# Self-attention's output projection as three float32r products, with in-place cosine products

## The reference

```python
q = (xn @ Wq).reshape(b, n, h, dh).transpose(0, 2, 1, 3)
k, v = split(xn @ Wkv)
q = q * cos + _rotate_half(q) * sin
k = k * cos + _rotate_half(k) * sin
attn = softmax(where(causal, neg, einsum('bhid,bjd->bhij', q * scale, k)))
out = einsum('bhij,bjd->bhid', attn, v).transpose(0, 2, 1, 3).reshape(b, n, h * dh)
x = x + out @ Wo                       # 2048 x 256: the output projection
x = x + cross_attention(layernorm(x), ctx)
x = x + ffn(layernorm(x))
```

## Time and profile before

| | |
|---|---|
| median of 3 runs | 1405.72 us (1403.78 to 1406.74) |
| the profiled execution | 1405.16 us, of which its span 1403.3 us |
| busy over the span | PE 1383.5 us (99%), PEld 1169.1, DVE 975.1 (69%), ACT 716.2 (51%), POOL 437.1 (31%) |
| block A | from 0 to about 362 us |
| block B | from 362.2 us to the end |
| output projection (L710) | 512 instructions, 32 for each of 16 pairs |

### The profile page before, as it was taken

How to read it: one execution, slowest core, us unless ns; L and a number is a source line. 1 busy time by engine, 2 the same in 40 slices (tenths; PEclk the granted TensorE clock), 3 DMA queues, 4 the chain that set the end, 5 groups by cost and what they waited for, 6 DMA issues and landing times.

```text
span 1403.3 us, 55347 instructions
## 1 busy us (share of the span) xinstructions
PE 1383.5 (99%) x25185; PEld 1169.1 (83%) x25185; DVE 975.1 (69%) x1824; ACT 716.2 (51%) x940; POOL 437.1 (31%) x433
## 2 busy tenths in 40 slices
PE   8999999999999999999999999999999999999997
PEld 6788888876788888888888888888888888888884
DVE  5776677666246768677777768677777767676766
ACT  3545445443455555555465555555465555555450
POOL 4333233222223233323333233323323233324310
PEclk9999999999999999999999999999999999999999
DMA  9100000000211121211212121211212121211100
GB/s 255 37 1 32 1 31 1 31 1 2 68 53 49 33 76 51 60 50 47 65 32 66 33 78 50 61 50 47 65 32 65 32 79 50 61 50 47 50 4 8
DMA packets 38923, 66.78 MB, mean 48 GB/s; under 512 B 3717, under 2 KB 36930, under 8 KB 38690
## 3 DMA queue, kind: packets, MB, share of 16 engines
q1 hardware_dynamic: 38690, 63.24, 15.7%
HBM read 61.40 MB, written 1.84 MB: 45 GB/s over the span
## 4 chain that ended last, share of the span: by engine, by line
PE 72%; DVE 2%; issue 0%; POOL 0%; DVEq 0%
PE proj_ps L1366 20%; PE proj_ps L1357 20%; PE score_ps L1384 14%; PE sum_ps L1409 13%; PE side_ps L1444 2%; PE side_ps L1458 1%; PE side_ps L1426 1%; PE side_ps L1451 1%; DVE amax L1245 0%; DVE hidden L1267 0%; DVE sig L1277 0%; DVE hidden L1278 0%; PE side_ps L1433 0%; DVE exps L1167 0%; DVE totals L1189 0%
## 5 line engine op out<-in xcount | busy, mean ns | idle before, releaser
L1119 ACT ACTIVATE exps<-score_ps 125x1792 f32<-125x1792 f32 x192 | 320.4, 1669 | 431.1 <-PE score_ps L1384 431.1
L1167 DVE TENSOR_SCALAR exps<-exps,top 125x896 f32<-125x896 f32 x384 | 288.1, 792 | 22.1 <-ACT exps L1119 17.5
L1384 PE MATMUL score_ps<-spread,keys 32*125 32x112 f32 x6144 | 219.0, 279 | 0.0
L1158 DVE COPY vals<-proj_ps 125x512 f32<-125x512 f32 x192 | 129.5, 688 | 116.6 <-PE proj_ps L1366 114.3
L1409 PEld LDWEIGHTS sum_ps<-exps,vals 125*32 125x32 f32 x12288 | 162.4, 110 | 46.9 <-issue 34.0
L1384 PEld LDWEIGHTS score_ps<-spread,keys 32*125 32x125 f32 x6144 | 184.8, 183 | 15.4 <-issue 0.3
L1409 PE MATMUL sum_ps<-exps,vals 125*32 125x56 f32 x12288 | 190.9, 214 | 0.0
L1049 POOL TENSOR_TENSOR low<-raw_early,high 128x500 fp32r<-128x500 f32 x64 | 84.5, 1322 | 216.8 <-PE proj_ps L1357 215.9
L1111 ACT ACTIVATE keys<-proj_ps,b_k 128x500 f32<-128x500 f32 x192 | 129.9, 677 | 23.7 <-PE proj_ps L1357 20.3
L1049 POOL TENSOR_TENSOR low_early<-raw_early,high_early 128x500 fp32r<-128x500 f32 x62 | 89.4, 1459 | 168.8 <-PE proj_ps L1357 168.8
L293 POOL TENSOR_TENSOR swapped<-swapped,sin 128x448 f32<-128x448 f32 (+1 forms) x72 | 86.0, 1198 | 126.5 <-ACT swapped L530 125.5
(11 more groups left out here) (169 smaller groups left out, 2415.2 us busy)
## 6 DMA issues: line engine op xcount, KB each, us to landing
raw_early<-in_ctxT SPq DMA_DIRECT2D x64, 500.0 KB, 4.1
raw<-in_ctxT SPq DMA_DIRECT2D x32, 500.0 KB, 3.6
w_q<-in_attn_Wq SPq DMA_DIRECT2D x4, 512.0 KB, 8.6
w_o<-in_attn_Wo SPq DMA_DIRECT2D x1, 2048.0 KB, 21.7
out<-y_out SPq DMA_DIRECT2D x16, 112.0 KB, 2.7
rows<-in_x SPq DMA_DIRECT2D x1, 1344.0 KB, 17.4
raw_early<-in_ffn_gate_wT SPq DMA_DIRECT2D x1, 1024.0 KB, 9.4
raw_early<-in_ffn_val_wT SPq DMA_DIRECT2D x1, 1024.0 KB, 5.1
```

What stands on the lines that cost most here:

```text
L1119: nc.scalar.activation(exps[t % 2][:, :, :, :].rearrange("p h r n -> p r h n"), score_ps[0:TILE, :, 0:2 * QW].rearrange("p r (h n) -> p r ...
L1158: nc.vector.tensor_copy(vals[r][:, 2 * q:2 * q + 2, :, 0:HD], proj_ps[q][0:TILE, :].rearrange("p (k h d) -> p k h d", k=2, d=HD))\
L1167: nc.vector.tensor_scalar(tile, tile, LIMIT_LO, top[:, n, at:at + 1], ALU.max, ALU.min)\
L1384: ins = nc.tensor.matmul(score_ps[0:TILE, r, to:to + HE * S], keys[c % 2][32 * r:32 * r + 32, k, (at + half) * TILE:(at + half + 1) * TILE ...
```

## The change

`outT` and `w_o` are each kept as two float32r tensors, a rounded half (`outT_h`, `w_oh`) and the rest (`outT_l`, `w_ol`), and the projection sums three products of them. ScalarE's `out_half` writes the rounded half, both batch rows of a half k one behind the other; a new step of VectorE, `out_low`, subtracts it from the bank, and that step now increases `outT_ready`. `attn_Wo` is loaded in three pieces into room that is unused until pair 2 (`queries`, `gate_q`), and in pair 0 ScalarE rounds it and VectorE takes the rest (`out_weights` on each). `cosines` writes its product straight into `qT` or `keyT`, and `rotated` adds in place; `by_cos` goes. To make room, the float32 cross-attention weights and the mask share the room of `w_q`, loaded after its last use; six parameters of block B are loaded at its start.

```diff
-        w_o = sb("w_o", [P, AH, D])
+        w_oh = sb("w_oh", [P, AH, D], F32R)
+        w_ol = sb("w_ol", [P, AH, D], F32R)
-        outT = sb("outT", [P, AH, ROWS])
+        outT_h = sb("outT_h", [P, AH, ROWS], F32R)
+        outT_l = sb("outT_l", [P, AH, ROWS], F32R)
...
             sp.wait_ge(raw_used, 3)
-            for c in range(2):
-                sp.dma_start(early.ring(c), context_chunk(dram, c)).then_inc(early_ctx_in[c], 16)
+            sp.dma_start(early.ring(0), context_chunk(dram, 0)).then_inc(early_ctx_in[0], 16)
+            sp.wait_ge(unit_filled, UNIT[("q", GROUPS - 1, AU - 1)] + 1)
+            for k, name in enumerate(("xattn_WkT", "xattn_WvT")):
+                sp.dma_start(early.w_f[:, k, :, :], dram[name].rearrange("(c p) n -> p c n", p=P)).then_inc(early_w_in, 16)
+            sp.dma_start(early.mask_i, dram["mask"]).then_inc(early_in, 16)
+            sp.dma_start(early.ring(1), context_chunk(dram, 1)).then_inc(early_ctx_in[1], 16)
...
                 else:
                     dve.wait_ge(swap_ready, r + 1)
-                if r >= 2:
-                    dve.wait_ge(rot_ready, r - 1)
-                chain.inc(nc.vector.tensor_tensor(by_row(by_cos[r % 2][:, 0:w]), by_row(bank(name)[:, 0:w]),
-                                                  cos[:, :].unsqueeze(1).to_broadcast([P, n, S]), ALU.mult))
-                chain.wait()
+                    nc.vector.tensor_tensor(qT[g % 2][:, name[2], :, :, 0:S].rearrange("p b h s -> p h b s"),
+                                            bank(name)[:, 0:2 * GR].rearrange("p (h b s) -> p h b s", h=2, s=S),
+                                            cos[:, :].unsqueeze(1).unsqueeze(1).to_broadcast([P, 2, GROUP, S]),
+                                            ALU.mult).then_inc(cos_ready, 1)
+                dve.wait_ge(cos_ready, r + 1)
                 nc.vector.sem_inc(free(name), 1)
...
+            def out_low(p, k, b):
+
+                dve.wait_ge(outT_high, 2 * (2 * p + k) + b + 1)
+                nc.vector.tensor_tensor(outT_l[:, AU * k:AU * (k + 1), b * S:(b + 1) * S],
+                                        out_ps[:, b, 0:AU * S].rearrange("p (h s) -> p h s", s=S),
+                                        outT_h[:, AU * k:AU * (k + 1), b * S:(b + 1) * S].bitcast(F32),
+                                        ALU.subtract).then_inc(outT_ready, 1)
+
+            def out_weights(n):
+
+                dve.wait_ge(wo_high, n + 1)
+                nc.vector.tensor_tensor(out_part(w_ol, n), out_raw(n), out_part(w_oh, n).bitcast(F32), ALU.subtract)\
+                  .then_inc(wo_low, 1)
...
                 if p:
                     norm2_rows(p - 1)
+                out_low(p, 0, 0)
+                out_low(p, 0, 1)
                 for name in more[3:4]:
                     rotary(name)
+                out_low(p, 1, 0)
+                out_low(p, 1, 1)
+                if p == 0:
+                    for n in range(len(O_PARTS)):
+                        out_weights(n)
...
+                if p == 0:
+                    for n in range(len(O_PARTS)):
+                        out_weights(n)
                 probs_out(p, 0)
                 for name in more[2:3]:
                     swap(name)
                 out_half(p, 0, 0)
+                out_half(p, 0, 1)
                 probs_out(p, 1)
-                out_half(p, 0, 1)
...
                 to = begin(("y", p))
-                pe.wait_ge(wo_in, 16)
+                pe.wait_ge(wo_low, len(O_PARTS))
                 pe.wait_ge(outT_ready, 4 * (p + 1))
                 for h in range(AH):
-                    ins = nc.tensor.matmul(to[0:ROWS, 0:D], outT[:, h, :], w_o[:, h, :], start=(h == 0),
-                                           stop=(h == AH - 1))
+                    for n, (x, w) in enumerate(((outT_h, w_oh), (outT_h, w_ol), (outT_l, w_oh))):
+                        ins = nc.tensor.matmul(to[0:ROWS, 0:D], x[:, h, :], w[:, h, :], start=(h == 0 and n == 0),
+                                               stop=(h == AH - 1 and n == 2))
```

More of the change, by code:

```diff
@@ L230, in block_a, with out_part, out_raw, wait_rotated @@
         ROT = {name: n for n, name in enumerate([name for name in units if name[0] in ("kv", "q")])}
+        O_PARTS = ((0, 8), (8, 14), (14, 16))
+        def out_part(w, n):
+            return w[:, O_PARTS[n][0]:O_PARTS[n][1], :].rearrange("p h n -> p (h n)")
+        def out_raw(n):
+            if n == 2:
+                return gate_q[:, 0, :].bitcast(F32)
+            return queries[:, :, :].rearrange("p c n -> p (c n)")[:, D * O_PARTS[n][0]:D * O_PARTS[n][1]]
+        def wait_rotated(eng, r):
+            eng.wait_ge(rot_ready, r + 1)
         def bank(name):
@@ L252, in _ @@
             sp.dma_start(rows[:, 2 * GP:PAIRS, :], x[:, 2 * GP:PAIRS, :]).then_inc(x_in[1], 16)
-            sp.dma_start(w_o[:, :, :], dram["attn_Wo"].rearrange("(h p) n -> p h n", p=P)).then_inc(wo_in, 16)
+            for n, (first, last) in enumerate(O_PARTS):
+                sp.dma_start(out_raw(n).rearrange("p (h n) -> p h n", n=D),
+                             dram["attn_Wo"].rearrange("(h p) n -> p h n", p=P)[:, first:last, :]).then_inc(wo_in, 16)
             sp.dma_start(w_xq[:, :, :], dram["xattn_WqT"].rearrange("(c p) n -> p c n", p=P)).then_inc(small2_in, 16)
@@ L262, in _ @@
                 if n == 0:
[L263 to L266, removed]
+                    sp.wait_ge(early_zero, 1)
                     for to, of in early.loads(dram):
@@ L550, in out_half, with out_weights @@
                 act.wait_ge(pv_done, 2 * p + k + 1)
-                ins = nc.scalar.copy(outT[:, AU * k:AU * (k + 1), b * S:(b + 1) * S],
-                                     out_ps[:, b, 0:AU * S].rearrange("p (h s) -> p h s", s=S))
-                ins.then_inc(outT_ready, 1)
+                nc.scalar.copy(outT_h[:, AU * k:AU * (k + 1), b * S:(b + 1) * S],
+                               out_ps[:, b, 0:AU * S].rearrange("p (h s) -> p h s", s=S)).then_inc(outT_high, 1)
+            def out_weights(n):
+                act.wait_ge(wo_in, 16 * len(O_PARTS))
+                nc.scalar.copy(out_part(w_oh, n), out_raw(n)).then_inc(wo_high, 1)
             def normed2_out(p):
@@ L667, in scores @@
                 g, j = divmod(p, GP)
-                pe.wait_ge(rot_ready, ROT[("kv", g)] + 1)
+                wait_rotated(pe, ROT[("kv", g)])
                 if p:
@@ L845, in __init__, with share @@
         self.res = sb("res", [ROWS, 1])
[L846 to L850, removed]
+    def share(self, room):
+        n = 2 * DC * D
+        self.w_f = room[:, 0:n].rearrange("p (k c n) -> p k c n", k=2, c=DC)
+        self.mask_i = room[0:TILE, n:n + BATCH * BT].bitcast(I32).rearrange("p (b t) -> p b t", b=BATCH)
     def ring(self, n):
@@ L855, in loads @@
     def loads(self, dram):
-        pairs = [(self.mask_i[:, :, :], dram["mask"]),
-                 (self.b_k[:, :], dram["xattn_bk"]),
+        pairs = [(self.b_k[:, :], dram["xattn_bk"]),
                  (self.head_of[:, :], dram["c_head_of"]),
@@ L1014, in _ @@
             load(2, 0, 2)
+            late = ((w_xo[:, :, :], dram["xattn_WoT"].rearrange("(a p) n -> p a n", p=P)),
+                    (ln_gamma[:, :], dram["xattn_gamma"].partition_broadcast(ROWS)),
+                    (ln_beta[:, :], dram["xattn_beta"].partition_broadcast(ROWS)),
+                    (gate_b[:, :], dram["ffn_gate_b"].partition_broadcast(ROWS)),
+                    (val_b[:, :], dram["ffn_val_b"].partition_broadcast(ROWS)),
+                    (out_b[:, :], dram["ffn_out_b"].partition_broadcast(ROWS)))
+            assert len(late) == N_LATE
+            for to, of in late:
+                sp.dma_start(to, of).then_inc(late_in, 16)
             def store(p):
```

56 lines of the change are left out of this document (28 added, 28 removed).

## The result

The changed kernel takes 1428.18 us (median of 4 runs, 1426.83 to 1428.37) against 1406.23 before: the ratio is 1.0164, 95% interval 1.0152 to 1.0177. It is slower, by about 22 us where the prediction said 14. The profiled execution took 1428.06 us with a span of 1426.3. Block B has hardly changed: its first product starts at 385.13 us (362.22 before), 22.9 of the 23.0 us by which the span grew. So the loss lies in block A.

A forecast was written before the change was run, and what follows sets the result against it. Block A is bounded by TensorE's own work list. First two pairs +8.5, pairs 2 to 13 +2.8, late pairs +3.8, pair 14 -1.1, pair 15 and end +0.5 make +14.5 on 1405.16: 1419.7, said as 1420 us, range 1408 to 1429.

The forecast's parts named there:

- The projection: TensorE's output projection: 48 float32r products take 5.76 us instead of 7.00, saving 1.24 us each time.
- The estimate of three quarters: Output projection by the skill's pass counts: 5.25 us, total some 8 us lower; the prediction used the slower measured pace.
- The wait in a regular pair: out_heads(p,1) waits 1.47 us for VectorE's two half-0 subtractions, resuming at T+6.57; net +0.23 us per pair.
- The late pairs: Pairs 3, 5, 7, 9: late VectorE lengthens the wait by 1.05 or 0.85 us, +3.8 us together.
- The first two pairs: Pairs 0 and 1: casting and subtracting the weights delays the start, +8.5 us with their projection's gain included.
- The clock's share: First projection's wait of some 4.7 us: a clock fall loses 1.7 us, half of it hidden, so +0.8 us.
- Pair 14: Pair without rotations: projection gains 1.24 us, wait grows by some 0.1 us; -1.1 us.
- Pair 15 and the end: Subtractions behind the 3.52 us norm2_rows delay out_heads(15,1) by 3.0 us; less two projection gains, +0.5 us.
- the term for the clock: Granted TensorE clock: +0.8 us counted in the first two pairs, nothing for the waits of later pairs.
- The clock falls in the new waits: Rival: TensorE's clock drops, 1.7 us at each of four wide waits, 1426.5 us; in all twelve 1440; chance 0.12.
- the waits of 1.95 and 2.93 us: TensorE waits in the earlier trace near 20.09 and 30.12 us: clock stayed at 1.00, respectively 0.66 over 5 us.
- the vanished wait: Rival: out_heads(p,1) has no wait for the half-0 subtractions in 12 pairs, price 17.6 us, 1402.1 us; chance 0.10.

The follow-up runs named there:

- e7: Changed kernel plus spare bf16 products on TensorE in the waits before out_heads(p,1), only in pairs 5, 7, 9 and 15; 1421.12 us, ratio 1.0115.
- e3: Kernel before the change with only the cosine products written in place into qT and keyT; 1403.9 us, ratio 0.9997.
- e2: Changed kernel plus spare bf16 products in the waits of pairs 1 to 13 and 15 and ahead of the first projection; 1420.29 us, ratio 1.0110.
- e1: Changed kernel with the two half-0 subtractions moved on VectorE ahead of the third rotation's sum and the row norm; 1401.04 us, ratio 0.9975.
- e6: Changed kernel without the product of the values' first part and the weights' second part (two of three products); 1433.7 us, ratio 1.0203.
- e8: e6 plus spare bf16 products: twelve in eight pairs with long waits, otherwise as in e2; 1422.52 us, ratio 1.0127.
- e5: e1 with the first projection in float32, the weights' subtraction cut into five pieces and two casts ahead of the pair loop; 1395.61 us, ratio 0.9935.
- e4: Kernel before with its float32 projection, plus a subtraction like out_low freeing the bank and ScalarE's two copies side by side; 1429.55 us, ratio 1.0176.

## Why the prediction was wrong in size and right in kind

- **The projection: right.** 5.69 to 5.72 us from its start to the turn at full clock, predicted 5.76. The estimate of three quarters by the passes of the Trainium skill (FP8 and Floating Point Precision, TensorE Precision Notes), 5.25 us, lies below every pair.
- **The wait in a regular pair: right** in place, cause and size: 1.45 to 1.47 us, released by `outT_l`, T+6.63 for T+6.57. A regular pair loses 0.23 to 0.26.
- **The late pairs: right but for the clock.** The waits are 2.46, 2.26, 2.46 and 2.26 us (predicted 2.3 to 2.5). Pair 3 loses 1.24 (0.23 + 1.05 predicted); pairs 5, 7 and 9 lose 1.45 to 1.6 more than that working gives, and e7 gives it back.
- **The first two pairs: +9.1 for +8.5, in part by luck:** against e3 it is +10.0. `less_max(1)` at 57.05 (57.3 predicted), `out_heads(1,1)` at 75.81 (74.4). The subtraction of the weights took the upper bound, 5.4 us from 51.64 to 57.05, not the 4.6 taken. The clock's share, predicted +0.8, is 0.8 to 1.2 by e2 and e7.
- **Pair 14: -0.7 for -1.1.** Its turn now waits 0.37 us for `normalise`; the working let the whole 1.24 through.
- **Pair 15 and the end: the wait right, its follow-up missed.** `norm2_rows` took 3.51 us again and the wait is 2.87 us. I had priced a wait of about 3 us, as long as the one of the earlier trace rows that I read as a fall, with no fall behind it.

**The step that failed** is the term for the clock: for the waits of the late pairs and of pair 15 the sum has nothing for what the clock does behind them (+3.8 and +0.5). It was left to the rival "The clock falls in the new waits", with the sentence that the four wide ones last "less than the 2.93" and a chance of 0.12. I drew a line between the waits of 1.95 and 2.93 us and put 2.3 to 2.5 on the harmless side. The trace of before had nothing in between, so it could not bear that. The runs showed falls after 2.26, 2.46 and 2.87 us, at 1.5 to 1.6 us each in pairs 5, 7 and 9 (1.7 was my price) and 2.5 in pair 15, in all 7.1 us by the medians of e7. With 0.6 more in the first pairs, 0.5 in the regular ones (most of it pair 4), 0.4 in pair 14 and 0.2 less at the end, 14.5 + 7.1 + 1.3 = 22.9. The time of that rival, 1426.5, was near, but by luck: it named pair 3, where the clock held, and not pair 15, where it fell. The Trainium skill (TensorE: Matmul & The Clock Gate, HAM oscillation) tells of a wait in every step that slows every step; pairs 5, 7, 9 and 15 went that way, pair 3 and the nine pairs with waits of 1.45 to 1.47 us did not.

The opposite rival, the vanished wait (1402.1), is what e1 makes true at 1401.04: its condition was the right one, VectorE being free of the two subtractions by about T+5.3, but the changed kernel does not meet it.

## What to carry to other kernels

A shorter product pays only as far as the next wait in line allows, so before costing it look at what the engine's following instruction waits for, and where in the other engine's list its releaser stands; e1 turns +22 us into -4 by moving two instructions past two. Price every new wait of the matrix engine also by what the clock does after it, with both outcomes in the range where the trace shows no wait of that length. When another engine turns out to be the later one (VectorE in eight pairs of e6 and e8), less work on TensorE does not pay there; in e8 each of those pairs lost 0.7 us or more.

## What the runs showed of the hardware

The clock's fall is not a matter of the wait's length alone: in pair 3 a wait of 2.46 us left the clock at 1.00 in the changed kernel and again in e7, while the same 2.46 us in pair 7 and 2.26 in pairs 5 and 9 brought it to 0.50. What tells pair 3 apart stays open; no run separated it. In e6 and e8 the turns of pairs 14 and 15 wait 2.23 to 2.24 us; the first product of `out_heads` behind them takes 1.02 us in pair 14 and 1.86 in pair 15. Even one and the same wait ends both ways. Ahead of the second group's keys TensorE waits 2.74 to 2.76 us in six traces; behind it the clock stays at 1.00 in the changed kernel, e2 and e7, and it falls to 0.50 within 1.5 us after the wait in e1, e5 and e8. The lines of e2 and e5:

```profile
30.46 1.02 PE L688 MATMUL unit_ps<-xnT,w_kv 128*128 128x224 f32 x4 [2.75 <-DVEq L397]
31.41 1.09 PE L693 MATMUL unit_ps<-w_kv,xnT 128*64 128x128 f32 x16
...
30.14 1.08 PE L719 MATMUL unit_ps<-xnT,w_kv 128*128 128x224 f32 x4 [2.75 <-DVEq L408]
31.15 1.98 PE L724 MATMUL unit_ps<-w_kv,xnT 128*64 128x128 f32 x16
```

The first two lines are e2, the last two e5: the 16 instructions that follow the first four take 1.09 us in one and 1.98 in the other. So a wait of this length can be given a price and a chance from these traces, but not a certain outcome. Of the waits of 1.45 to 1.47 us, in nine pairs of the changed kernel and thirteen of e4, none was followed by a fall.
